# A token tower on one core: maxima rows by column transfers, k and q in one part, six of sixteen score slots written ahead by ScalarE, normalisation on VectorE in two pieces

## The chip, the core and the metric

The kernel runs on one core of a Trainium2 chip. Five engines work side by side: TensorE (PE, with its weight loads as PEld), VectorE (DVE), ScalarE (ACT), GpSimd (POOL) and SyncE (SP), which here only issues transfers. They share SBUF; TensorE writes to PSUM, which VectorE and ScalarE read. Each engine runs its own instructions in order and waits for the others by semaphores. The metric is the time of one execution in microseconds on the device, as the median of several.

## The reference

The input is 2 x 1024 token ids. What is computed, cut to what matters:

```
h = relu(conv(embedding(x)))                      # 2 x 1024 x 128
x = layernorm(h)
q, k, v = x Wq, x Wk, x Wv                        # 8 heads of 64
dots = q k^T * 64**-0.5
h = h + (softmax(dots) v) Wo + x
m = layernorm(h)
a = (layernorm(m) * g + b) Wa + ba + m
y = fc2_e(gelu(fc1_e(a)))                         # expert e by the token's place, 8 experts
h = h + gelu(y Wn + bn)
```

The softmax is the part around the change: each query's scores less their maximum over the keys go into the exponential.

## The kernel before

**Steps, parts, units.** A step s (0 to 7) is one pair of heads of one batch row. It has 16 units `(s, kc, half)`: key block kc (128 keys, 0 to 7) against query half (512 queries), both heads side by side, 128 x 1024 numbers in one PSUM slot. A step is worked in eight parts, two units in each; parts 0 to 3 take the query half 0, parts 4 to 7 the half 1 (`units_of`). In a part TensorE runs, in this order (`part_items`): a maximum item, two score items ("exp"), a second maximum item, what stands beside (`beside_values`), and then the values of the two units of the part before ("pv", line 524, into `acc_o`).

**Slots.** Three PSUM slots of two banks each go round all items that need one. Item n takes slot n % 3, and TensorE waits until the item three places earlier is released (line 572, `release`): an exp item by ScalarE's exponential (line 692), a maximum item by VectorE's reduction (line 847), a k or q item by VectorE's remainder (line 842).

**Scores** (`scores`, line 512) are four terms, each of two matmuls, one for each head: k_round x q_round, k_round x q_rest, k_rest x q_round and, as the fourth, a row of ones against `neg_rows`, which holds the negated maximum of each query. The sum is in PSUM when ScalarE takes the exponential.

**Maxima.** They are made a step ahead: "max" items multiply q_round with k_round (line 447), transposed, so that queries are partitions, and VectorE reduces along the keys (line 847). When four query blocks are done VectorE joins the two key halves into `maxes` (line 852, 128 x 8, both operands in SBUF). That happens in part 5 (for the next step, half 0) and in part 1 (for this step, half 1). A "rows" item, in parts 6 and 2, turns them: two transposes on TensorE (line 454), a negated copy by VectorE (`neg_max`, line 859), and two transfers on SP's queue (line 349) into the rows of `neg_rows`.

**k and q** of the next step are projected in part 0 (k) and part 1 (q): six matmuls each (line 440), rounded by ScalarE (line 697), remainder by VectorE (line 842).

**Denominators.** GpSimd adds up the exponentials (`add`, line 1026, 14 additions of 128 x 1024 a step). In part 3 TensorE sums step s - 1 over the partitions ("den", line 535), ScalarE copies (line 702), SP spreads the copy over 128 partitions (line 334), VectorE inverts (`invert`, line 880, last in its part 4), SP stores to DRAM (line 336) and loads it back, each row to 64 partitions (line 341, two transfers). GpSimd multiplies `attn_out` by it (`normalise`, line 1016) between its additions for kc 5 and 6 of half 1. Step 7's denominators come as "last den", one item for each half (lines 543, 871, 874).

**SP's queue** is one list, in order: the row transfers of half 1, the spread and its loads, the row transfers of the next step's half 0. In step 4 the first four experts' weights (line 355, 2 MB) stand between the first and the second of these; in step 6 the other four stand ahead of the last.

**Step 7** has, besides, the feed-forward layer's start: "wo" (line 462), the layer norm on VectorE (line 911), "nt" (line 469, which waits for it) and "xa". Behind it come the experts (lines 602, 613, 621).

The functions that the change touches, and what calls them:

Of the kernel before, what the change touches and what calls it, by code (L numbers as in the profile page):

```python
# [19 lines left out]
F32 = mybir.dt.float32  # L20
# [7 lines left out]
B, S = 2, 1024  # L28
# [23 lines left out]
AHEAD, ROWS_AT = 12, 9  # L52
# [7 lines left out]
PROLOGUE = ([("k", 0), ("q", 0)] + [("max", *m) for m in MAXES[:ROWS_AT]] + [("rows", 0, 0)]  # L60
            + [("max", *m) for m in MAXES[ROWS_AT:AHEAD]])
# [6 lines left out]
FFN_ITEMS = {(STEPS - 1, 0): [("wo",)], (STEPS - 1, 3): [("nt",)], (STEPS - 1, 5): [("xa",)], (STEPS - 1, 6): [("last den", 0)]}  # L68

# [18 lines left out]


def part_items(s, part):  # L90
# [3 lines left out]
    items += [("exp", *u) for u in units_of(s, part)] + maxes[1:] + beside_values(s, part)  # L94
# [19 lines left out]
NO_SLOT = ("pv", "o", "inv", "norms")  # L114
# [21 lines left out]
def unit(s, kc, half):  # L136

    return s * UNITS + half * KCH + kc

# [6 lines left out]
def build(nc, x, tables, w_in, wo_in, small_in, next_b, fc_in, out):  # L146
    VOCAB = VOCAB_ROWS
    with ExitStack() as ctx:
# [42 lines left out]
        with ExitStack() as att:  # L191
# [5 lines left out]
            def operands(p, scope):  # L197

                return [sb(f"{name}{p}", [128, S], F32R, scope) for name in ("q_round", "q_rest", "k_round", "k_rest", "neg_rows")]
# [3 lines left out]
            maxes = sb("maxes", [128, 2, KCH], F32, att)  # L203
            neg_max = sb("neg_max", [GROUP, 2, CHUNK], F32R, att)
            one_rows = sb("one_rows", [128, CHUNK], F32R, att)
            odd_operands = operands(1, att)

            with ExitStack() as early:
                xR = sb("xR", [C, B * S], F32R, early)
                xL = sb("xL", [C, B * S], F32R, early)  # L210
                q_round, q_rest, k_round, k_rest, neg_rows = zip(operands(0, early), odd_operands)
# [60 lines left out]
        rows_made = sem("rows_made")  # L272
        rows_loaded = sem("rows_loaded")
        summed = [[sem(f"summed_{p}_{half}") for half in ("low", "high")] for p in ("even", "odd")]
# [18 lines left out]
        def release(item):  # L293
# [8 lines left out]
            if kind == "rows":  # L302
                return rows_made, 2 * item[1] + item[2] + 1
# [12 lines left out]
        duo_slots, late_slot = (slots[FIRST_SLOT], slots[SUMS_SLOT]), slots[LATE_SLOT]  # L316
        inv_dram = nc.dram_tensor("inv_scratch", [128, 2 * S // 128], F32, kind="Internal").ap()
# [4 lines left out]
        def _(sp):  # L322
# [8 lines left out]
            def spread(s):  # L331
# [6 lines left out]
                if s > 0:  # L338
                    sp.wait_ge(normalised, s)
# [40 lines left out]
        def _(pe):  # L380
# [50 lines left out]
            def prep_item(item, slot):  # L431
# [10 lines left out]
                elif kind == "max":  # L442
# [7 lines left out]
                else:  # L450
                    half = item[2]
                    pe.wait_ge(max_joined, 2 * v + half + 1)
                    for h in range(2):
                        last = pe.transpose(slot[0:GROUP, h * BANK:h * BANK + CHUNK], maxes[:, h, half * GROUP:(half + 1) * GROUP],  # L454
                                            ident[:, :])
# [28 lines left out]
            def ffn_item(item, slot):  # L484

                kind = item[0]
                if kind == "wo":
                    pe.wait_ge(normalised, PAIRS)
# [11 lines left out]
            def scores(item, slot):  # L500
# [64 lines left out]
            for s in range(STEPS):  # L565
                for item, n in numbered(STEP_ITEMS[s], FIRST[s]):
# [5 lines left out]
                    pe.wait_ge(*release(ALL_ITEMS[n - SLOTS]))  # L572
# [55 lines left out]
            for half in range(2):  # L628
                pe.wait_ge(normalised, STEPS + half)
# [17 lines left out]
        def _(act):  # L647
# [85 lines left out]

            def o_copy(s, half):
# [18 lines left out]
            for s in range(STEPS):  # L753
                for item, n in numbered(STEP_ITEMS[s], FIRST[s]):
                    if item[0] == "o":
# [39 lines left out]
        def _(dve):  # L795
# [39 lines left out]
            def dve_item(item, n):  # L835
# [8 lines left out]
                elif kind == "max":  # L844
# [4 lines left out]
                    if qc % GROUP == GROUP - 1 and keys == 1:  # L849
                        own = slice(qc - GROUP + 1, qc + 1)  # L850
                        dve.wait_ge(maxed, MAXES.index(item[1:]) + 1)
                        dve.tensor_tensor(maxes[:, :, own], half_maxes[:, :, own, 0], half_maxes[:, :, own, 1],  # L852
                                          ALU.max).then_inc(max_joined, 1)
                elif kind == "rows":
                    _, v, half = item
                    dve.wait_ge(filled, n + 1)
                    if v + half > 0:
                        dve.wait_ge(rows_loaded, 32 * (2 * v + half))
                    dve.tensor_scalar(neg_max[:, :, :], slot[0:GROUP, :].rearrange("c (h n) -> c h n", h=2)[:, :, 0:CHUNK],
                                      -1.0, None, ALU.mult).then_inc(rows_made, 1)  # L860
# [4 lines left out]
                elif kind == "last den":  # L865
# [4 lines left out]
                    dve.wait_ge(normalised, STEPS - 1 + half)  # L870
# [42 lines left out]

            def dve_step(s):
                for item, n in numbered(STEP_ITEMS[s], FIRST[s]):
                    if item[0] == "inv":
                        invert(item[1])
# [172 lines left out]
```

## Time and profile before

| | us |
|---|---|
| median of 3 runs | 442.79 (442.66 to 442.96) |
| the profiled execution | 443.59 |
| its span, first to last instruction | 441.7 |

| engine | busy us | share of the span | instructions |
|---|---|---|---|
| PE | 417.8 | 95% | 2654 |
| PEld | 249.5 | 56% | 2654 |
| DVE | 252.7 | 57% | 327 |
| ACT | 204.5 | 46% | 285 |
| POOL | 300.8 | 68% | 148 |

The granted clock was 0.984 of full speed over the span. The time of matmuls overlaps: one pair begins before the last has ended, so neither the busy time nor the mean of one matmul is what a further one costs; the distance between starts is.

### The profile page before, as it was taken

Reading aid. Unit: us, or ns where it says so; the run is one execution under the profiler, and the core shown is the slowest. Engines: PE = TensorE matmul, PEld = TensorE weight load, DVE = VectorE, ACT = ScalarE, POOL = GpSimd, SP = SyncE. Lnnn points to the kernel's source line nnn. Section 1 sums busy time; section 2 is a strip of 40 time slices with the busy share of each in tenths; the row PEclk is TensorE's granted clock in tenths of the full one; section 3 lists DMA queues with packets and bytes.
Section 4 is the critical chain, followed back from the end, with each engine's and each line's share of the span. In section 5 each row is a group of like instructions: output and inputs, shape, how many; then the busy total and the mean of one; then the engine's idle time right before and its main releaser. Section 6 shows DMA issues by size and latency. Waiting matters only on the chain.

```text
span 441.7 us, 6550 instructions
## 1 busy us (share of the span) xinstructions
PE 417.8 (95%) x2654; PEld 249.5 (56%) x2654; DVE 252.7 (57%) x327; ACT 204.5 (46%) x285; POOL 300.8 (68%) x148
## 2 busy tenths in 40 slices
PE   7798899999999999999999999999999789697995
PEld 7675555555555455445544555454557335286994
DVE  1777675665658466755746575666654940356121
ACT  1455535354545445444544445454442634333663
POOL 3070278978898889879987988998794936900111
PEclk9989999999999999999999999999999979989999
DMA  6000000000100010020051000100330010000011
GB/s 228 1 1 1 0 2 1 2 0 3 49 2 0 3 48 1 2 49 2 1 193 48 2 0 3 48 2 0 100 142 0 2 48 4 0 1 1 19 30 49
DMA packets 7962, 12.03 MB, mean 27 GB/s; under 512 B 2684, under 2 KB 5244, under 8 KB 7932
## 3 DMA queue, kind: packets, MB, share of 16 engines
q1 hardware_dynamic: 7356, 10.63, 7.9%
q10 hardware_dynamic: 576, 0.98, 0.7%
q8 instruction: 21, 0.34, 0.3%
q14 instruction: 9, 0.07, 0.1%
HBM read 10.38 MB, written 1.11 MB: 26 GB/s over the span
## 4 chain that ended last, share of the span: by engine, by line
PE 85%; DVE 6%; POOL 2%; ACT 2%; issue 2%; DMA 1%; POOLq 0%; SPq 0%; ACTq 0%; DVEq 0%
PE acc_o L524 25%; PE slot L512 25%; PE slot L447 9%; PE slot L440 6%; PE slot L462 3%; PE slot L602 3%; PE acc_o L423 3%; PE acc_o L613 2%; DVE normed L911 2%; POOL sums L1026 2%; PE slot L535 2%; DMA residual<-in_x 1%; PE slot L454 1%; PE slot L478 1%; PE slot L399 1%
## 5 line engine op out<-in xcount | busy, mean ns | idle before, releaser
L1026 POOL TENSOR_TENSOR sums<-sums,probs 128x1024 f32<-128x1024 f32 x96 | 228.9, 2384 | 38.3 <-ACT probs L692 28.1
L847 DVE TENSOR_REDUCE half_maxes<-slot 128x2 f32<-128x1024 f32 x128 | 156.5, 1225 | 96.5 <-PE slot L447 96.1
L692 ACT ACTIVATE probs<-slot 128x1024 f32<-128x1024 f32 x128 | 124.9, 1025 | 131.4 <-PE slot L512 131.4
L524 PE MATMUL acc_o<-probs,v_all 128*64 128x512 f32 x512 | 124.1, 606 | 0.0
L524 PEld LDWEIGHTS acc_o<-probs,v_all 128*64 128x64 f32 x512 | 31.3, 136 | 60.4 <-issue 45.1
L1026 POOL TENSOR_TENSOR sums<-probs 128x1024 f32<-128x1024 f32 x16 | 38.2, 2389 | 32.3 <-ACT probs L692 32.3
L447 PE MATMUL slot<-k_round,q_round 64*128 64x512 f32 x256 | 57.7, 449 | 0.7 <-DVE half_maxes L847 0.7
L447 PEld LDWEIGHTS slot<-k_round,q_round 64*128 64x128 f32 x256 | 23.8, 183 | 53.2 <-issue 46.9
L512 PE MATMUL slot<-q_round,k_round 64*128 64x512 f32 x256 | 51.4, 397 | 1.2 <-DVE k_rest L842 1.0
L512 PE MATMUL slot<-q_round,k_rest 64*128 64x512 f32 x256 | 50.5, 390 | 0.0
L512 PE MATMUL slot<-q_rest,k_round 64*128 64x512 f32 x256 | 50.5, 390 | 0.0
L512 PE MATMUL slot<-neg_rows,one_rows 64*128 64x512 f32 x256 | 50.4, 388 | 0.0
L1042 POOL TENSOR_TENSOR probs<-probs,residual 128x256 f32<-128x256 f32 x8 | 5.8, 725 | 46.8 <-ACT probs L778 46.8
L512 PEld LDWEIGHTS slot<-q_round,k_round 64*128 64x128 f32 x256 | 24.1, 185 | 10.0 <-issue 4.9
L512 PEld LDWEIGHTS slot<-neg_rows,one_rows 64*128 64x128 f32 x256 | 24.1, 184 | 5.5
L512 PEld LDWEIGHTS slot<-q_round,k_rest 64*128 64x128 f32 x256 | 24.1, 184 | 5.5
L512 PEld LDWEIGHTS slot<-q_rest,k_round 64*128 64x128 f32 x256 | 24.1, 184 | 5.1
L771 ACT ACTIVATE probs<-slot,small 128x128 f32<-128x128 f32 x64 | 17.4, 383 | 18.1 <-PE slot L602 18.1
L871 DVE RECIPROCAL inv_sb<-slot 128x512 f32<-128x512 f32 x2 | 6.7, 3358 | 25.2 <-POOL attn_out L1016 22.5
L740 ACT COPY attn_out<-acc_o 128x512 f32<-128x512 f32 x14 | 8.2, 588 | 21.2 <-PE acc_o L524 21.2
L852 DVE TENSOR_TENSOR maxes<-half_maxes 128x8 f32<-128x8 f32 x16 | 17.6, 1103 | 0.6
L1016 POOL TENSOR_TENSOR attn_out<-attn_out,inv_sb 128x1024 f32<-128x1024 f32 x7 | 16.6, 2377 | 0.0
(114 smaller groups left out, 412.6 us busy)
## 6 DMA issues: line engine op xcount, KB each, us to landing
inv_sb<-inv_scratch SPq DMA_DIRECT2D x14, 256.0 KB, 3.9
v_all<-in_fc SPq DMA_DIRECT2D x4, 512.0 KB, 4.9
fc_late<-in_fc SPq DMA_DIRECT2D x4, 512.0 KB, 6.3
residual<-in_x SPq DMA_DIRECT2D x2, 512.0 KB, 5.9
out_h<-probs SPq DMA_DIRECT2D x8, 128.0 KB, 1.8
v_all<-in_w ACTq DMA_DIRECT2D x3, 256.0 KB, 7.4
neg_rows<-neg_max SPq DMA_DIRECT2D x32, 2.0 KB
woT<-in_wo SPq DMA_DIRECT2D x1, 256.0 KB, 7.7
```

The lines of the kernel that those rows point to most:

```text
L423: last = pe.matmul(bank(6 + t % 2), xs[:, rows], ws[:, :], start=(i == 0), stop=(i == 2))
L440: last = pe.matmul(slot[:, half * BANK:(half + 1) * BANK], ws[:, w, v % PAIRS, :], xs[:, cols], start=(i == 0), stop=(i == 2))
L447: last = pe.matmul(slot[:, h * BANK:(h + 1) * BANK], q_round[p][head_rows(h), qc * CHUNK:(qc + 1) * CHUNK], k_round[p][head_rows(h), half ...
L462: last = pe.matmul(slot[:, j * C:(j + 1) * C], attn_out[:, b * PAIRS + r, j * CHUNK:(j + 1) * CHUNK], woT[:, r, :], start=(r == 0), stop=( ...
L512: last = pe.matmul(slot[:, h * BANK:(h + 1) * BANK], stationary, qs[head_rows(h), cols], start=(i == 0), stop=(i == 3))
L524: last = pe.matmul(acc_o[head_rows(h), cols], v_all[:, s, kc, head_rows(h)], probs[unit(s, kc, half) % TILES][:, h, :], start=(kc == 0), s ...
L692: act.activation(probs[u % TILES][:, :, :].rearrange("p h n -> p (h n)"), slot[:, :], ACT.Exp, scale=SCALE).then_inc(exped, 1)
L771: act.activation(hidT[d % 2][:, i, r, :], slot[:, i, r], ACT.Gelu, bias=fc1_b_col[:, e * HC + r:e * HC + r + 1]).then_inc(hid_made, 1)
L847: dve.reduce_max(half_maxes[:, :, qc, keys], slot[:, :].rearrange("p (h n) -> p h n", h=2), AX.X).then_inc(maxed, 1)
L852: dve.tensor_tensor(maxes[:, :, own], half_maxes[:, :, own, 0], half_maxes[:, :, own, 1], ALU.max).then_inc(max_joined, 1)
L1016: pool.tensor_tensor(attn_out[:, s, :], attn_out[:, s, :], inv_sb[:, :], ALU.mult).then_inc(normalised, 1)
L1026: pool.tensor_tensor(sums[s % 2][half][:, :, :], before[:, :, :], probs[kc][:, :, :], ALU.add).then_inc(summed[s % 2][half], 1)
```

## The change

- **Rows by columns.** The "rows" items go, with their transposes, the copy by VectorE and `neg_max`. SP waits for the join and sends each column of `maxes` (128 numbers, one a partition) to its stretch of a row: eight transfers for each half instead of two. The row holds the maxima themselves, and the constant row is -1 instead of 1.
- **A plane.** When the eight have landed, SP stores the half's two rows to DRAM, waits, and loads them to all 128 partitions: `max_planes`, 128 x 1024. Both stand on SP's queue behind the columns, each behind a wait for the one before it.
- **Six of sixteen slots ahead.** For kc 2, 4, 6 of each half ScalarE writes minus the plane into the unit's slot ("fill"), at the end of the part before and behind that part's two exponentials. TensorE waits for it instead of for the slot's release, and runs three terms that add to it. It holds where the item three places earlier is an exp, max, k or q item: 47 units (six a step, five in step 7, in which (7, 2, half 1) keeps four terms).
- **k and q in one part.** Both stand in part 0.
- **Normalisation on VectorE.** GpSimd's 128 x 1024 multiplication is now two of 128 x 512 on VectorE, behind the second maximum of parts 5 and 7, and in step 7 both in part 6.

The diff, cut to its core:

```diff
-PROLOGUE = ([("k", 0), ("q", 0)] + [("max", *m) for m in MAXES[:ROWS_AT]] + [("rows", 0, 0)]
-            + [("max", *m) for m in MAXES[ROWS_AT:AHEAD]])
+PROLOGUE = [("k", 0), ("q", 0)] + [("max", *m) for m in MAXES[:AHEAD]]
...
+PREFILLED = (2, 4, 6)
...
-    if part < 2 and s + 1 < STEPS:
-        items.append(("kq"[part], s + 1))
-    if part == 2:
-        items.append(("rows", s, 1))
+    if part == 0 and s + 1 < STEPS:
+        items += [("k", s + 1), ("q", s + 1)]
     if part == 3 and s > 0:
         items.append(("den", s - 1))
-    if part == 6 and s + 1 < STEPS:
-        items.append(("rows", s + 1, 0))
...
-    items += [("exp", *u) for u in units_of(s, part)] + maxes[1:] + beside_values(s, part)
+    items += [("exp", *u) for u in units_of(s, part)] + maxes[1:]
+    beside = beside_values(s, part)
+    if s > 0:
+        items += [("norm", s - 1, i) for i, p in enumerate((5, 7) if s + 1 < STEPS else (6, 6)) if p == part]
+    items += beside
+    if part % 4 < 3:
+        items.append(("fill", *units_of(s, part + 1)[0]))
...
+WHOLE_SLOT = ("exp", "max", "k", "q")
+FILLED = [item[1:] for n, item in enumerate(ALL_ITEMS)
+          if item[0] == "exp" and item[2] in PREFILLED and ALL_ITEMS[n - SLOTS][0] in WHOLE_SLOT]
...
-                sp.wait_ge(rows_made, 2 * v + half + 1)
+                i = 2 * v + half
+                sp.wait_ge(max_joined, i + 1)
+                if i > 0:
+                    sp.wait_ge(rows_loaded, ROW_COUNT * i)
                 for h in range(2):
-                    sp.dma_start(neg_rows[v % 2][h * D:h * D + 1, half * BANK:(half + 1) * BANK].bitcast(F32)
-                                 .rearrange("a (c n) -> a c n", c=GROUP), neg_max[:, h, :].bitcast(F32)).then_inc(rows_loaded, 16)
+                    for c in range(GROUP):
+                        qc = half * GROUP + c
+                        sp.dma_start(max_rows_of[v % 2][h * D:h * D + 1, qc * CHUNK:(qc + 1) * CHUNK].bitcast(F32),
+                                     maxes[:, h, qc:qc + 1].bitcast(F32)).then_inc(rows_loaded, 16)
+                sp.wait_ge(rows_loaded, ROW_COUNT * (i + 1))
+                if i > 1:
+                    sp.wait_ge(plane_loaded, 16 * (i - 1))
+                sp.dma_start(rows_dram[half], max_rows_of[v % 2][0:128:D, half * BANK:(half + 1) * BANK].bitcast(F32)).then_inc(rows_stored, 16)
+                sp.wait_ge(rows_stored, 16 * i + 16)
+                if i > 1:
+                    sp.wait_ge(filled_in, filled_up_to(i - 2))
+                sp.dma_start(max_planes[half][:, :], rows_dram[half:half + 1].rearrange("a h n -> a (h n)").partition_broadcast(128)
+                             .rearrange("p a n -> p (a n)")).then_inc(plane_loaded, 16)
...
-                terms = ((k_round[p], q_round[p]), (k_round[p], q_rest[p]), (k_rest[p], q_round[p]), (one_rows, neg_rows[p]))
+                terms = [(k_round[p], q_round[p]), (k_round[p], q_rest[p]), (k_rest[p], q_round[p])]
+                ahead = item[1:] in FILLED
+                if not ahead:
+                    terms.append((minus_rows, max_rows_of[p]))
                 for i, (ks, qs) in enumerate(terms):
                     if i == 3 and kc == 0:
-                        pe.wait_ge(rows_loaded, 32 * (2 * s + half + 1))
+                        pe.wait_ge(rows_loaded, ROW_COUNT * (2 * s + half + 1))
                     for h in range(2):
                         stationary = ks[head_rows(h), :] if i == 3 else ks[head_rows(h), keys]
                         last = pe.matmul(slot[:, h * BANK:(h + 1) * BANK], stationary, qs[head_rows(h), cols],
-                                         start=(i == 0), stop=(i == 3))
+                                         start=(i == 0 and not ahead), stop=(i == len(terms) - 1), skip_group_check=ahead)
...
+                    if item[0] == "exp" and item[1:] in FILLED:
+                        pe.wait_ge(filled_in, FILLED.index(item[1:]) + 1)
+                    else:
+                        pe.wait_ge(*release(ALL_ITEMS[n - SLOTS]))
...
+            def fill(unit_item):
+
+                _, s, kc, half = unit_item
+                n = ALL_ITEMS.index(("exp", s, kc, half))
+                act.wait_ge(*release(ALL_ITEMS[n - SLOTS]))
+                act.wait_ge(plane_loaded, 16 * (2 * s + half) + 16)
+                act.activation(slots[n % SLOTS][:, :], max_planes[half][:, :], ACT.Copy, scale=-1.0).then_inc(filled_in, 1)
...
+                        turn = 2 * v + qc // GROUP
                         dve.wait_ge(maxed, MAXES.index(item[1:]) + 1)
+                        if turn > 1:
+                            dve.wait_ge(rows_loaded, ROW_COUNT * (turn - 1))
...
-                elif kind == "rows":
-                    _, v, half = item
-                    dve.wait_ge(filled, n + 1)
-                    if v + half > 0:
-                        dve.wait_ge(rows_loaded, 32 * (2 * v + half))
-                    dve.tensor_scalar(neg_max[:, :, :], slot[0:GROUP, :].rearrange("c (h n) -> c h n", h=2)[:, :, 0:CHUNK],
-                                      -1.0, None, ALU.mult).then_inc(rows_made, 1)
...
+            def normalise(s, half):
+
+                cols = slice(half * BANK, (half + 1) * BANK)
+                dve.wait_ge(inv_loaded, s * 32 + 32)
+                dve.tensor_tensor(attn_out[:, s, cols], attn_out[:, s, cols], inv_sb[:, cols], ALU.mult).then_inc(normalised, 1)
...
-            def normalise(s):
-
-                pool.wait_ge(inv_loaded, s * 32 + 32)
-                pool.tensor_tensor(attn_out[:, s, :], attn_out[:, s, :], inv_sb[:, :], ALU.mult).then_inc(normalised, 1)
...
-                        if half == 1 and kc == 5 and s > 0:
-                            normalise(s - 1)
...
```

## Rows read from the trace of the kernel before

**Rows 1.** The page, part 1 of PE and part 4 by engine

```profile
PE 417.8 (95%) x2654; PEld 249.5 (56%) x2654; DVE 252.7 (57%) x327; ACT 204.5 (46%) x285; POOL 300.8 (68%) x148
PE 85%; DVE 6%; POOL 2%; ACT 2%; issue 2%; DMA 1%; POOLq 0%; SPq 0%; ACTq 0%; DVEq 0%
```

**Rows 2.** Timeline, PE, step 3, part 4: start us, duration us, engine, line

```profile
189.43 0.50 PE L447 MATMUL slot<-k_round,q_round 64*128 64x512 f32 x2
189.76 0.39 PE L512 MATMUL slot<-q_round,k_round 64*128 64x512 f32 x2
190.68 0.40 PE L512 MATMUL slot<-q_round,k_round 64*128 64x512 f32 x2
191.91 1.94 PE L524 MATMUL acc_o<-probs,v_all 128*64 128x512 f32 x8
193.78 0.50 PE L447 MATMUL slot<-k_round,q_round 64*128 64x512 f32 x2
```

**Rows 3.** Timeline, PE: first maxima of parts 6, 7 and then 0, 1

```profile
198.14 0.50 PE L447 MATMUL slot<-k_round,q_round 64*128 64x512 f32 x2
202.88 0.50 PE L447 MATMUL slot<-k_round,q_round 64*128 64x512 f32 x2
207.27 0.51 PE L447 MATMUL slot<-k_round,q_round 64*128 64x512 f32 x2
213.25 0.50 PE L447 MATMUL slot<-k_round,q_round 64*128 64x512 f32 x2
```

**Rows 4.** Timeline, ACT in part 4 of step 3

```profile
190.90 1.94 ACT L692 ACTIVATE probs<-slot 128x1024 f32<-128x1024 f32 x2 [2.61 <-PE slot L512]
```

**Rows 5.** Timeline, DVE in parts 4 and 5 of step 3

```profile
193.17 0.24 DVE L880 RECIPROCAL inv_flat<-den_flat 128x16 f32<-128x16 f32 x1
...
196.38 1.23 DVE L847 TENSOR_REDUCE half_maxes<-slot 128x2 f32<-128x1024 f32 x1 [0.83 <-PE slot L447]
197.65 1.10 DVE L852 TENSOR_TENSOR maxes<-half_maxes 128x8 f32<-128x8 f32 x1
```

**Rows 6.** Timeline, POOL in parts 4 to 6 of step 3

```profile
192.91 2.39 POOL L1026 TENSOR_TENSOR sums<-probs 128x1024 f32<-128x1024 f32 x1 [1.07 <-ACT probs L692]
196.35 9.96 POOL L1026 TENSOR_TENSOR sums<-sums,probs 128x1024 f32<-128x1024 f32 x4 [1.05 <-ACT probs L692]
```

**Rows 7.** Timeline, SP's queue in parts 4 and 5 of step 3

```profile
188.31 0.57 SPq L334 DMA_DIRECT2D den_flat<-den_sb  x1
193.44 0.32 SPq L336 DMA_DIRECT2D inv_scratch<-inv_flat  x1
194.85 1.14 SPq L341 DMA_DIRECT2D inv_sb<-inv_scratch  x2
```

**Rows 8.** Issue to landing: page, part 6; tile v_all, SP's loads

```profile
inv_sb<-inv_scratch SPq DMA_DIRECT2D x14, 256.0 KB, 3.9
DMA to landing us min/median/max: 3.6/4.9/6.3
```

**Rows 9.** Line 852, DVE's join: duration ns min/median/max

```profile
L852 DVE TENSOR_TENSOR maxes<-half_maxes x16: 168/1102/2154, 42.0 to 343.9; 128x8 f32<-128x8 f32 x16
```

**Rows 10.** Timeline, SP's queue in step 4

```profile
224.72 1.86 SPq L355 DMA_DIRECT2D v_all<-in_fc  x4
```

**Rows 11.** Timeline, DVE and PE at the start of step 0

```profile
42.00 0.17 DVE L852 TENSOR_TENSOR maxes<-half_maxes 128x8 f32<-128x8 f32 x1
48.87 0.41 PE L512 MATMUL slot<-neg_rows,one_rows 64*128 64x512 f32 x2
```

**Rows 12.** Timeline, step 7 and its end

```profile
354.92 1.94 PE L535 MATMUL slot<-sums,ones 128*32 128x512 f32 x8 [4.22 <-DVE neg_max L859]
379.63 2.37 POOL L1016 TENSOR_TENSOR attn_out<-attn_out,inv_sb 128x1024 f32<-128x1024 f32 x1
382.10 3.36 DVE L871 RECIPROCAL inv_sb<-slot 128x512 f32<-128x512 f32 x1 [22.45 <-POOL attn_out L1016]
386.93 1.97 PE L543 MATMUL slot<-sums,ones 128*64 128x512 f32 x4 [4.05 <-POOL sums L1026]
```

More of the change, by code:

```diff
@@ L51 @@
 MAXES = [(v, qc, keys) for v in range(STEPS) for qc in range(KCH) for keys in range(2)]
-AHEAD, ROWS_AT = 12, 9
+AHEAD = 12
+ROW_COUNT = 16 * 2 * GROUP
 WARM_START, WARM_SPLIT = 24, 10
@@ L111, in step_items @@
     return items
-NO_SLOT = ("pv", "o", "inv", "norms")
+NO_SLOT = ("pv", "o", "inv", "norms", "norm", "fill")
 def numbered(items, first):
@@ L138, in unit, with filled_up_to @@
     return s * UNITS + half * KCH + kc
+WHOLE_SLOT = ("exp", "max", "k", "q")
+FILLED = [item[1:] for n, item in enumerate(ALL_ITEMS)
+          if item[0] == "exp" and item[2] in PREFILLED and ALL_ITEMS[n - SLOTS][0] in WHOLE_SLOT]
+def filled_up_to(turn):
+    return len([u for u in FILLED if 2 * u[0] + u[2] <= turn])
 def adds_done(s, kc):
@@ L197, in operands @@
             def operands(p, scope):
-                return [sb(f"{name}{p}", [128, S], F32R, scope) for name in ("q_round", "q_rest", "k_round", "k_rest", "neg_rows")]
+                return [sb(f"{name}{p}", [128, S], F32R, scope) for name in ("q_round", "q_rest", "k_round", "k_rest", "max_rows_of")]
             probs = [sb(f"probs{i}", [128, 2, BANK], F32, att) for i in range(TILES)]
             half_maxes = sb("half_maxes", [128, 2, KCH, 2], F32, att)
-            maxes = sb("maxes", [128, 2, KCH], F32, att)
-            neg_max = sb("neg_max", [GROUP, 2, CHUNK], F32R, att)
-            one_rows = sb("one_rows", [128, CHUNK], F32R, att)
+            maxes = sb("maxes", [128, 2, KCH], F32R, att)
+            max_planes = [sb(f"max_plane{i}", [128, 2 * BANK], F32, att) for i in range(2)]
+            minus_rows = sb("minus_rows", [128, CHUNK], F32R, att)
             odd_operands = operands(1, att)
@@ L210, in build @@
                 xL = sb("xL", [C, B * S], F32R, early)
-                q_round, q_rest, k_round, k_rest, neg_rows = zip(operands(0, early), odd_operands)
+                q_round, q_rest, k_round, k_rest, max_rows_of = zip(operands(0, early), odd_operands)
                 wR = sb("wR", [C, 2, PAIRS, 2 * D], F32R, early)
@@ L301, in release @@
                 return maxed, MAXES.index(item[1:]) + 1
-            if kind == "rows":
-                return rows_made, 2 * item[1] + item[2] + 1
             if kind == "wo":
@@ L338, in spread @@
                 if s > 0:
-                    sp.wait_ge(normalised, s)
+                    sp.wait_ge(normalised, 2 * s)
                 for h in range(2):
@@ L449, in prep_item @@
                                          k_round[p][head_rows(h), half * BANK:(half + 1) * BANK], start=True, stop=True)
[L450 to L455, printed above, removed]
                 last.then_inc(filled, 1)
@@ L628, in _ @@
             for half in range(2):
-                pe.wait_ge(normalised, STEPS + half)
+                pe.wait_ge(normalised, 2 * STEPS - 1 + half)
                 wo_half(1, half, late_slot).then_inc(wo_filled, 1)
@@ L754, in _ @@
                 for item, n in numbered(STEP_ITEMS[s], FIRST[s]):
-                    if item[0] == "o":
+                    if item[0] == "fill" and item[1:] in FILLED:
+                        fill(item)
+                    elif item[0] == "o":
                         o_copy(item[1], item[2])
@@ L869, in dve_item @@
                     dve.wait_ge(filled, n + 1)
-                    dve.wait_ge(normalised, STEPS - 1 + half)
+                    dve.wait_ge(normalised, 2 * (STEPS - 1) + half)
                     dve.reciprocal(inv_sb[:, cols], slot[:, 0:BANK]).then_inc(inverted, 1)
@@ L917, in dve_step @@
                         invert(item[1])
+                    elif item[0] == "norm":
+                        normalise(item[1], item[2])
                     elif item[0] == "norms":
```

14 lines of the change are left out of this document (7 added, 7 removed).

## The prediction

> **What bounds the kernel now.** I read the page's parts 1 and 4 first: TensorE is busy 95% of the span and is 85% of the chain that ended last [rows 1]. So a gain must come out of TensorE's list, and a loss comes from whatever makes it wait. What a matmul costs there I take from the timeline, since matmuls overlap. In part 4 of step 3 one score item follows the other after 190.68 - 189.76 = 0.92 us, for four terms [rows 2]: a term costs 0.23 us, though one of its matmuls lasts 0.39. The part lasts 193.78 - 189.43 = 4.35 us. Parts with more in them [rows 3]: part 6, which has a rows item, 4.74 us, so the item costs 0.39; part 0, which has k, 5.98 us. Then the timelines of the other engines in the same stretch [rows 4 to 7], to see how much room each has before TensorE needs it. I count in times from the start of the part: ScalarE's two exponentials run from 1.47 to 3.41 [rows 2, 4]; VectorE inverts the denominators at 3.74 [rows 2, 5].
>
> **What TensorE saves.** In each of steps 1 to 6: six fourth terms, 6 x 0.23 = 1.4 us, and two rows items, 0.8 us. That is 2.1 us of 40 (part 5 of one step to part 5 of the next). k and q side by side cost what they cost apart.
>
> **Does the fill come in time?** One row of an ordinary part answers. With three terms in its first score item the exponentials end at about 3.2 (the second waits for its own scores), and a copy of 128 x 1024 costs ScalarE about what an exponential does, 0.97 us [rows 4]: ready at 4.2. TensorE wants the slot 0.33 us [rows 2] into the next part, which begins at 4.12, so at 4.45. It is hidden, with 0.2 us to spare; if the copy cost 1.3 us it would cost 0.1 us, 47 times, 5 us. In part 0 the fill stands behind q's rounding; by the same counting it is 0.1 us late. VectorE has both remainders there too; with that I put down 0.2 us a step.
>
> **The plane.** Half 1's maxima are joined in part 1, some 12.4 us into the step. The issue of a row transfer takes SP about 0.57 us (the spread's [rows 7] is the nearest, 128 pieces too), so eight take 4.6; the store of the inverse took from its issue to the next issue 194.85 - 193.44 = 1.4 us [rows 7]; 512 KB landed 3.6 to 6.3 us after issue, where four such loads stood together [rows 8], the first soonest. So the rows are there at 12.4 + 4.6 + 1.4 = 18.4, the plane at 18.4 + 1.4 + 3.6 = 23.4. The first use of the row is at 22.1, that of the plane (end of part 4's exponentials) at 24.5. Both fit; the plane has 1 us. SP comes to the spread at 20.4 instead of 19.9, and the spread lands behind the plane, at 23.5 to 24; VectorE wants it at 24.8. If columns cost more, this is where it shows. Taken: nothing in steps 1 to 6. For half 0 there is 5 us more.
>
> **The normalisation, where the gain goes.** In the kernel before, GpSimd did it late in the half, and nobody waited. Now VectorE does, in its own list, behind the join of part 5, and ahead of part 6's first maximum. Behind the waiting instruction stands that maximum, and for its slot TensorE waits with part 6's second maximum item. Counted from the start of part 5 (193.78):
> - The inverse is asked for at 194.85 and 195.42 and lands 3.9 us later [rows 7, 8]: at 5.5. These steps hang on the inversion, which VectorE does at the same place as before, so this does not move.
> - GpSimd: the addition of kc 2 starts 2.57 into the part, behind the exponential [rows 6]; with three terms 2.3. One lasts 2.4, four in a row 9.96 [rows 6], so 2.49 apart: they end at 4.7 and 7.2.
> - VectorE's join starts at 3.87 and lasts 1.10, until 4.97, just when GpSimd's addition ends (196.35 + 2.39 = 198.74, and 197.65 + 1.10 = 198.75) [rows 5, 6]. The shortest join lasts 0.17 us, the longest 2.15, for the same eight numbers [rows 9]. I read this as a wait for GpSimd's running addition, which an operation with two operands in SBUF has to make. The normalisation is such an operation.
> - So it misses the gap at 4.7, starts at 7.2, takes between 0.5 and 0.7 (a 128 x 512 operation; half of the 1.23 of 128 x 1024 [rows 5]), and the maximum behind it ends at 7.2 + 0.6 + 1.23 = 9.0. TensorE wants the slot 6.05 into the part (4.12 + 0.33 + 1.6). It waits **3.0 us**.
>
> The second piece, in part 7, has its inverse but can meet an addition as well; I count 0.3 us at part 0's second maximum. Bounds of both together: 0.5 us, if the inverse lands before 4.7, to 5.4, if each meets a whole addition.
>
> The Trainium skill says the same of the lock ("SBUF — State Buffer", section "Who interferes with whom"): a `tensor_tensor` with both inputs in SBUF contends with GpSimd's reads, and the later one fully blocks. It speaks against this change. By that rule the stall is the 3.0 us above and the sum that of the forecast; without it the time is that of the second rival. The trace agrees, by the joins of 0.17 to 2.15 us.
>
> **Steps 1 to 6:** -2.1 + 3.0 + 0.3 + 0.2 = +1.4 us each, six times +8.4.
>
> **Step 4** more: the 2 MB of experts stood before the spread already, issued from 224.72 [rows 10]. They now stand behind the plane, 3 us later in the step, and land, with up to 6.3 us for one [rows 8], about 28.3 into it; the spread lands behind them, while VectorE waits at the inversion from 24.8. It holds part 5's maxima, and TensorE waits 2.5 us (0 to 3.5).
>
> **Step 0.** The first join ends at 42.17, the fourth term of the first unit ran at 48.87 [rows 11], and would run 0.3 earlier. Columns: 42.2 + 4.8 + 1.4 = 48.4, just in time. The first plane lands at 53.4, before ScalarE can use it; half 1's plane comes about 1 us late. Of 2.3 us of savings 1.0 us is left.
>
> **Step 7 and the end.** TensorE waited 4.22 us for the negated copy, which stood behind the second layer norm on VectorE, and then ran the denominators for 1.94 us [rows 12] and "nt", which needs that norm. Without the copy the denominators run inside the wait, and "nt" begins about 2.2 us sooner. At the end the chain goes through GpSimd's last additions, in which its normalisation of 2.37 us stood [rows 12], between two of them; TensorE's last sum at 386.93 waited for the additions. It is gone: 2.4 us. With one term, 0.2: -4.8 us. The 22.45 us for which VectorE waited there [rows 12] are no gain beyond this, since the next on the chain is the last sum.
>
> **Sum:** -1.0 + 8.4 + 2.5 - 4.8 = +5.1. The profiled execution has a span of 441.7 and took 443.59; the median of the runs is 442.79, 0.8 below. From the median: **447.9 us**.
>
> **Rivals.**
> 1. *The inverse is in time.* If it lands before the addition of kc 2 ends, join and normalisation share a gap: 0.5 us instead of 3.0, and with the phase so shifted the piece in part 7 is free. Then -1.4 a step, -8.4: in all -11.7, **431 us**. For it: 5.5 against 4.7 is close. Against: even with the second load landing 3.5 us after its issue it is 5.1. Chance 0.17.
> 2. *No lock for this operation.* VectorE waits for the inverse only: 5.5 + 0.7 + 1.23 = 7.5, stall 1.4; -0.5 a step: **437 us**. For it: the join is tiny, and could wait for its own operands instead. Against: its end falls on the addition's end. Chance 0.08.
> 3. *TensorE saves it all*, because the landing is earlier than I read or the wait has more room: about -18, **425 us**. Chance 0.09.
> 4. *The columns are slow* (slower still). They are pieces of 4 bytes, where the spread's have 64. It decides from 1 us more for the chain of eight on: at 2 us more TensorE waits 0.7 us a step at the first filled unit of half 1, +5, **453 us**; at 4 us more 2.7 a step, 467. Nothing in the trace shows such pieces. Chance 0.16.
> 5. *It does nothing*: gains and waits cancel within 0.2%, which is about what a measurement of this kernel can tell. The forecast's sum is 5 us of terms that are 8 and 5 large. Chance 0.05.
>
> The forecast keeps 0.45. Range: 430 to 457 leaves out most of 3 (0.09) and the far part of 4 (0.07) and a few hundredths on the near side, under 0.2. Its own range for the forecast is 443.5 to 452. Faster 0.17 + 0.08 + 0.09 + 0.01 = 0.35, same 0.05, slower 0.6.
>
> **What would show it.** The distance of two "den" items (L535) in the timeline, 40.0 now: 41.4 by the forecast, 38.6 by the first rival, 37.9 by the third. Who waited for whom: TensorE on the reductions of line 847, six times about 3 us, at part 6's second maximum. VectorE's normalisation: a mean well above 0.7 us, with its end on the end of an addition. Behind the loads of the planes, VectorE's inversion without a wait save in step 4. On ScalarE a fill of about 1.0 us. If TensorE waits for fills instead, the columns or the copy were mis-sized; if it waits for nothing and the step is 38 us, the wait for the inverse was.

## The result and the profile after

| | before | after |
|---|---|---|
| median, us | 442.79 (442.54 to 442.96, 5 runs) | 449.04 (447.11 to 449.66, 5 runs) |
| ratio | | 1.0129, 95% interval 1.0115 to 1.0144 |
| the profiled execution, us | 443.59 | 447.11 |
| its span, us | 441.7 | 445.3 |

Slower by 1.3%, with less work on TensorE: busy 405.0 us instead of 417.8 [rows 1]. The profiled execution is the fastest of the five, 1.9 us below the median. The page of the changed kernel, parts 1, 4, 5 and 6 (line, engine, operation, output and input, count; busy us, mean ns of one; idle us before it and what ended that; at the end the transfers' KB and us to landing):

```profile
PE 405.0 (91%) x2528; PEld 241.3 (54%) x2528; DVE 266.3 (60%) x325; ACT 251.0 (56%) x332; POOL 287.8 (65%) x141
PE 66%; DVE 12%; DMA 11%; SPq 3%; ACT 3%; POOL 2%; issue 2%; POOLq 0%; ACTq 0%
...
L476 PE MATMUL slot<-k_round,q_round 64*128 64x512 f32 x256 | 59.8, 466 | 19.7 <-DVE half_maxes L886 19.5
L769 ACT ACTIVATE slot<-max_plane 128x1024 f32<-128x1024 f32 x47 | 48.3, 1028 | 3.4 <-DMA max_plane<-rows_scratch 1.7
L953 DVE TENSOR_TENSOR attn_out<-attn_out,inv_sb 128x512 f32<-128x512 f32 x14 | 22.9, 1642 | 16.3 <-DMA inv_sb<-inv_scratch 16.3
...
max_plane<-rows_scratch SPq DMA_DIRECT2D x16, 512.0 KB, 3.5
inv_sb<-inv_scratch SPq DMA_DIRECT2D x14, 256.0 KB, 3.9
max_rows_of<-maxes SPq DMA_DIRECT2D x128, 0.5 KB, 2.0
```

The chain has moved: TensorE had 85% of it [rows 1], now 66; VectorE has 12% and transfers 11%, the loads of the inverse foremost. TensorE waits for VectorE's maxima (L886), 19.5 us in all. The piece of the normalisation (L953) lasts 1.64 us in the mean, and for the same 128 x 512 0.69 where nothing is in its way (below).

The place itself, in step 3, parts 5 and 6, from the timelines of TensorE, VectorE, GpSimd and SP's queue:

```profile
192.81 0.50 PE L476 MATMUL slot<-k_round,q_round 64*128 64x512 f32 x2
...
196.97 0.50 PE L476 MATMUL slot<-k_round,q_round 64*128 64x512 f32 x2
...
201.81 0.51 PE L476 MATMUL slot<-k_round,q_round 64*128 64x512 f32 x2 [2.73 <-DVE half_maxes L886]
```

```profile
196.48 1.10 DVE L894 TENSOR_TENSOR maxes<-half_maxes 128x8 fp32r<-128x8 f32 x1
198.47 2.15 DVE L953 TENSOR_TENSOR attn_out<-attn_out,inv_sb 128x512 f32<-128x512 f32 x1 [0.90 <-DMA inv_sb<-inv_scratch]
200.55 1.21 DVE L886 TENSOR_REDUCE half_maxes<-slot 128x2 f32<-128x1024 f32 x1
...
195.17 10.18 POOL L1064 TENSOR_TENSOR sums<-sums,probs 128x1024 f32<-128x1024 f32 x4 [0.51 <-ACT probs L721]
...
193.91 1.15 SPq L355 DMA_DIRECT2D inv_sb<-inv_scratch  x2
```

Part 5 starts at 192.81. GpSimd's additions start at 195.17 and stand some 2.5 apart, so there are gaps at about 197.6 and 200.1. The join ends at 197.58, in the first. The inverse lands at 198.47, 5.66 into the part, too late for that gap; the piece ends at 200.6, in the next. Then comes part 6's first maximum, until 201.76, and TensorE, which wanted its slot 2.73 us before, goes on at 201.81. The same wait, 2.70 to 2.73 us, stands in steps 1, 2, 3, 5 and 6. It is the gap that sets it, and not how late the inverse is: in step 2 the inverse landed 1.2 us later (6.9 into the part), just ahead of the same gap. The piece then took only 0.89 us and TensorE waited as long (VectorE and TensorE, step 2):

```profile
158.84 0.89 DVE L953 TENSOR_TENSOR attn_out<-attn_out,inv_sb 128x512 f32<-128x512 f32 x1 [2.15 <-DMA inv_sb<-inv_scratch]
160.92 0.49 PE L476 MATMUL slot<-k_round,q_round 64*128 64x512 f32 x2 [2.71 <-DVE half_maxes L886]
```

From den item to den item (TensorE's timeline; 40.0 us from each to the next up to step 6 before):

| stretch | before | after | difference | forecast |
|---|---|---|---|---|
| start to step 1's | 106.6 | 102.4 | -4.2 | -1.9 |
| 1 to 2 | 40.0 | 42.3 | +2.3 | +1.4 |
| 2 to 3, 3 to 4 | 80.0 | 81.8 | +1.8 | +2.8 |
| 4 to 5 | 40.0 | 46.3 | +6.3 | +3.9 |
| 5 to 6 | 40.0 | 42.5 | +2.5 | +1.4 |
| 6 to the end | 135.1 | 130.1 | -5.1 | -2.5 |
| sum | 441.7 | 445.3 | +3.6 | +5.1 |

The sum is that of the two profiled executions. The medians are 6.2 us apart, and no trace shows the other 2.6.

### The profile page after: what moved, and what is told of

The parts are those of the page before. It is cut to its first block, busy times and chain, and to the rows that moved or that the text cites. A ratio compares the mean times of both kernels' runs of the same rounds, so it can differ in the third digit from the quotient of the medians.

```text
span 445.3 us, 6537 instructions
## 1 busy us (share of the span) xinstructions
PE 405.0 (91%) x2528; PEld 241.3 (54%) x2528; DVE 266.3 (60%) x325; ACT 251.0 (56%) x332; POOL 287.8 (65%) x141
## 4 chain that ended last, share of the span: by engine, by line
PE 66%; DVE 12%; DMA 11%; SPq 3%; ACT 3%; POOL 2%; issue 2%; POOLq 0%; ACTq 0%
PE acc_o L550 18%; PE slot L538 17%; PE slot L476 8%; DMA inv_sb<-inv_scratch 6%; PE slot L468 5%; DVE half_maxes L886 4%; PE slot L485 3%; PE slot L631 3%; PE acc_o L642 2%; DVE attn_out L953 2%; POOL sums L1064 2%; DVE normed L946 2%; SPq L368 2%; DMA inv_scratch<-inv_flat 2%; PE acc_o L412 2%
## 5 line engine op out<-in xcount | busy, mean ns | idle before, releaser
L1064 POOL TENSOR_TENSOR sums<-sums,probs 128x1024 f32<-128x1024 f32 x96 | 232.0, 2417 | 68.1 <-ACT probs L721 57.5
L886 DVE TENSOR_REDUCE half_maxes<-slot 128x2 f32<-128x1024 f32 x128 | 156.3, 1224 | 81.8 <-PE slot L476 81.5
L721 ACT ACTIVATE probs<-slot 128x1024 f32<-128x1024 f32 x128 | 124.5, 1024 | 110.4 <-PE slot L538 110.4
L550 PE MATMUL acc_o<-probs,v_all 128*64 128x512 f32 x512 | 127.3, 620 | 0.0
L476 PE MATMUL slot<-k_round,q_round 64*128 64x512 f32 x256 | 59.8, 466 | 19.7 <-DVE half_maxes L886 19.5
L1064 POOL TENSOR_TENSOR sums<-probs 128x1024 f32<-128x1024 f32 x16 | 38.2, 2390 | 19.0 <-ACT probs L721 18.3
L769 ACT ACTIVATE slot<-max_plane 128x1024 f32<-128x1024 f32 x47 | 48.3, 1028 | 3.4 <-DMA max_plane<-rows_scratch 1.7
L953 DVE TENSOR_TENSOR attn_out<-attn_out,inv_sb 128x512 f32<-128x512 f32 x14 | 22.9, 1642 | 16.3 <-DMA inv_sb<-inv_scratch 16.3
L538 PE MATMUL slot<-max_rows_of,minus_rows 64*128 64x512 f32 x162 | 32.1, 390 | 0.3 <-DMA max_rows_of<-maxes 0.3
L538 PEld LDWEIGHTS slot<-max_rows_of,minus_rows 64*128 64x128 f32 x162 | 15.3, 184 | 4.0 <-DMA max_rows_of<-maxes 0.8
L881 DVE TENSOR_TENSOR k_rest<-slot,k_round 128x1024 fp32r<-128x1024 f32 x8 | 9.8, 1225 | 10.0 <-ACT k_round L726 9.9
L894 DVE TENSOR_TENSOR maxes<-half_maxes 128x8 fp32r<-128x8 f32 x16 | 15.1, 945 | 0.6
```

What stands on the lines that cost most here:

```text
L476: last = pe.matmul(slot[:, h * BANK:(h + 1) * BANK], q_round[p][head_rows(h), qc * CHUNK:(qc + 1) * CHUNK], k_round[p][head_rows(h), half ...
L550: last = pe.matmul(acc_o[head_rows(h), cols], v_all[:, s, kc, head_rows(h)], probs[unit(s, kc, half) % TILES][:, h, :], start=(kc == 0), s ...
L721: act.activation(probs[u % TILES][:, :, :].rearrange("p h n -> p (h n)"), slot[:, :], ACT.Exp, scale=SCALE).then_inc(exped, 1)
L769: act.activation(slots[n % SLOTS][:, :], max_planes[half][:, :], ACT.Copy, scale=-1.0).then_inc(filled_in, 1)
L886: dve.reduce_max(half_maxes[:, :, qc, keys], slot[:, :].rearrange("p (h n) -> p h n", h=2), AX.X).then_inc(maxed, 1)
L953: dve.tensor_tensor(attn_out[:, s, cols], attn_out[:, s, cols], inv_sb[:, cols], ALU.mult).then_inc(normalised, 1)
```

## The experiments

The theory: VectorE's piece in part 5 costs the time, by the late inverse and GpSimd's running addition together. The rivals: one of these two alone; the columns, planes and fills; for step 4 the transfers' traffic. The kernel before, run beside them, took 442.7 to 442.8 us; the ratios are against it.

**Normalisation back on GpSimd.**

```diff
-                        normalise(item[1], item[2])
+                        pass
...
+            def normalise(s):
+                pool.wait_ge(inv_loaded, s * 32 + 32)
+                pool.tensor_tensor(attn_out[:, s, :], attn_out[:, s, :], inv_sb[:, :], ALU.mult).then_inc(normalised, 2)
...
+                        if half == 1 and kc == 5 and s > 0:
+                            normalise(s - 1)
```

(VectorE passes over its two pieces, GpSimd has the multiplication back.)

> The changed kernel with the normalisation back on GpSimd as one 128 x 1024 multiplication behind kc 5 of half 1; columns, planes, filled slots and k with q stay. Theory (VectorE's piece in part 5, late inverse and GpSimd's addition, holds part 6's first maximum and with it TensorE): the waits of 2.7 us at part 6 are gone in steps 1 to 3 and 5 and 6, and in step 4 its second one of 2.0; the distance of two den items falls from 40.9 to 38.0; step 4's first wait (experts ahead of the spread) stays; GpSimd's 2.4 us come back at the end. 449.0 - 13.6 - 2.0 - 4.5 (slow clock behind the waits) + 2.4 = about 431 us. Rival (columns, planes and fills cost what the change loses): the steps stay at 40 to 41, 440 us or more.

Measured: 431.8 us, ratio 0.972 (0.966 to 0.978). The den distance is 37.7 us in four of five steps (44.3 in step 4), 38.0 was expected, 37.9 by the prediction's third rival; no wait at part 6 is left. TensorE's wait in part 5 of step 4 stays (2.97 us), and behind it the granted clock was 0.50 over 4 us. So the rest of the change works as computed, and 17 us lie in the place of the normalisation.

**The lock alone, taken away.**

```diff
-                dve.tensor_tensor(attn_out[:, s, cols], attn_out[:, s, cols], inv_sb[:, cols], ALU.mult).then_inc(normalised, 1)
+                dve.reduce_max(norm_dummy[:, ...], inv_sb[:, cols]..., AX.X).then_inc(normalised, 1)
```

> The multiplication is left out: in its place, at the same place and behind the same wait for the inverse, stands a reduction of 128 x 512 from SBUF, with one operand; attention is not normalised, except in step 7. Theory (an operation with two operands in SBUF waits for GpSimd's running addition): the piece lasts about 0.6 us instead of 2, TensorE's wait at part 6 falls from 2.7 to 1.3 us, part 7's piece costs nothing; five steps x 1.4, fewer stretches at the slow clock: 439 to 442 us. Rival (only the late inverse matters): the piece still ends with GpSimd's addition or costs as much, 449 us as before.

Measured: 436.8 us, ratio 0.985 (0.980 to 0.990). VectorE's and TensorE's timelines in step 3:

```profile
194.91 0.69 DVE L954 TENSOR_REDUCE norm_dummy<-inv_sb 128x2 f32<-128x512 f32 x1 [0.91 <-DMA inv_sb<-inv_scratch]
...
196.78 0.50 PE L477 MATMUL slot<-k_round,q_round 64*128 64x512 f32 x2 [1.26 <-DVE half_maxes L887]
```

With one operand in SBUF the piece lasts 0.69 us behind the same wait for the inverse, and TensorE's wait is 1.26 to 1.93 us. The rival "only the late inverse" falls: the second operand, of both pieces together, is worth 12 us.

**The inverse alone, taken away.**

```diff
-                    sp.wait_ge(normalised, 2 * s)
+                    sp.wait_ge(inv_loaded, 32 * s)
...
-                dve.wait_ge(inv_loaded, s * 32 + 32)
-                dve.tensor_tensor(..., attn_out[:, s, cols], inv_sb[:, cols], ALU.mult)
+                if s == STEPS - 2:
+                    dve.wait_ge(inv_loaded, s * 32 + 32)
+                dve.tensor_tensor(..., attn_out[:, s, cols], fixed[:, cols], ALU.mult)
```

> The pieces multiply by a fixed tile instead of the inverse and wait for no transfer (step 6's wait alone stays, since inv_sb is written behind it); attention is not normalised, except in step 7. Theory: the piece goes in the same gap between two additions as the join, part 6's wait falls from 2.7 to about 0.4 us, also in step 4, where only part 5's wait of 3 us stays: 449.0 - 5 x 2.3 - 2.0 - 4.3 = about 431 us. Rival (the lock alone makes the wait, whatever the inverse does): the piece waits for a whole addition still, 449 us. Rival (columns or fills): 440 us or more.

Measured: 430.4 us, ratio 0.972 (0.967 to 0.977). VectorE's timeline in step 3:

```profile
191.26 0.68 DVE L955 TENSOR_TENSOR attn_out<-attn_out,fixed 128x512 f32<-128x512 f32 x1
```

Both operands are in SBUF, GpSimd adds on, and the piece lasts 0.68 us: it follows the join in the same gap. Of the wait at part 6 0.28 us is left (den distance 38.2). The rival "the lock makes the wait, whatever the inverse does" falls too. It needs both.

**The real inverse, sooner.** VectorE inverts behind the first maximum of part 4 and no longer behind the second.

```diff
-    items = maxes[:1]
+    items = maxes[:1] + [("inv", s - 1)] * (part == 4 and s > 0)
```

(and "inv" no longer at the end of part 4)

> VectorE inverts behind the first maximum of part 4 instead of behind the second, 2.0 us sooner; nothing else. Theory: the inverse lands 3.6 us into part 5, ahead of the gap at 4.7, so join and piece share it; part 6's wait falls from 2.7 to about 0.4 us, the den distance from 40.9 to 38.6. In step 4 the inversion waits for the experts' transfers and now holds part 4's second maximum, 2 us more than before. About 434 us. Rival (the wait is GpSimd's addition whatever the inverse does, or columns and fills): 445 us or more.

Measured: 439.2 us, ratio 0.991 (0.988 to 0.995); 434 was expected, a miss by 5. The profiled execution took 443.8 us and holds both cases. VectorE and TensorE in step 2, and then in step 5:

```profile
157.65 1.07 DVE L894 TENSOR_TENSOR maxes<-half_maxes 128x8 fp32r<-128x8 f32 x1
158.79 0.69 DVE L953 TENSOR_TENSOR attn_out<-attn_out,inv_sb 128x512 f32<-128x512 f32 x1
...
160.68 0.51 PE L476 MATMUL slot<-k_round,q_round 64*128 64x512 f32 x2 [0.42 <-DVE half_maxes L886]
...
275.03 0.25 DVE L915 RECIPROCAL inv_flat<-den_flat 128x16 f32<-128x16 f32 x1 [0.83 <-DMA den_flat<-den_sb]
280.43 1.09 DVE L894 TENSOR_TENSOR maxes<-half_maxes 128x8 fp32r<-128x8 f32 x1
281.70 2.88 DVE L953 TENSOR_TENSOR attn_out<-attn_out,inv_sb 128x512 f32<-128x512 f32 x1 [0.17 <-DMA inv_sb<-inv_scratch]
...
285.76 0.80 PE L476 MATMUL slot<-k_round,q_round 64*128 64x512 f32 x2 [2.73 <-DVE half_maxes L886]
```

Where the inverse was there when the join ended, the piece took 0.69 us and TensorE waited 0.42; where it came 0.17 us late, the piece took 2.88 and TensorE waited 2.73. That happened in steps 1, 5 and 6 (late by 0.66, 0.17 and 0.34 us). The price of being late is a wait until the next gap, however small the lateness. My expectation had the landing at 3.6 into part 5 and the gap at 4.7. In those three steps it landed at 4.9 to 5.4. What failed is the 2 us: the denominators' spread had not landed where VectorE now wanted it, so the inversion waited 0.7 to 1.1 us in steps 1, 2, 3, 5 and 6, and came only 0.9 to 1.3 us sooner. That left next to nothing of the margin, and the scatter of the landing decided. In step 4 the inversion waited 7.68 us, and TensorE 3.96 instead of the changed kernel's 3.06. How many steps are late in an execution of 439 us no trace shows.

**The first piece one part later.**

```diff
-        items += [... enumerate((5, 7) if s + 1 < STEPS else (6, 6)) if p == part]
+        items += [... enumerate((6, 7) if s + 1 < STEPS else (6, 6)) if p == part]
```

> The changed kernel with the first piece of the normalisation one part later, behind part 6's second maximum, when the inverse has landed long since. Theory (late inverse and GpSimd's addition both count): no wait for the inverse, but the piece meets a running addition, ends with it and holds part 7's first maximum: TensorE waits some 1.2 us at part 7's second maximum instead of 2.7 at part 6's. 449.0 - 5 x 1.5 - 2.0 (step 4) - 4.3 (slow clock) = about 435 us. Rival (only the inverse is late): no wait, 429 us. Rival (columns, planes, fills): 445 us or more.

Measured: 438.9 us, ratio 0.990 (0.988 to 0.993). The timeline in step 3:

```profile
198.17 2.65 DVE L953 TENSOR_TENSOR attn_out<-attn_out,inv_sb 128x512 f32<-128x512 f32 x1
...
202.01 0.50 PE L476 MATMUL slot<-k_round,q_round 64*128 64x512 f32 x2 [1.10 <-DVE half_maxes L886]
```

Without any wait for the inverse the piece lasts 2.65 us, and TensorE waits 1.10 us, as expected; I had not counted that the second piece then lasts 2.40 and costs 0.6 more in each step (den distance 39.9).

**This one part of the change on the kernel before.** The edit is that of the change's own diff for the two pieces and what waits for them, and nothing else of it.

> The kernel before with this one part of the change alone: GpSimd's normalisation becomes VectorE's two pieces in parts 5 and 7 (in step 7 both in part 6). Theory: the same wait appears, 2.6 to 3 us at part 6 of each of six steps, den distance 42.6 or more instead of 40.0; 2.4 us gained at the end: 442.8 + 6 x 2.8 - 2.4 + up to 4 for the slow clock behind the waits = 457 to 461 us. Rival (the pieces only hurt together with filled slots and planes): 443 us or less.

Measured: 465.8 us, ratio 1.052 (1.049 to 1.055), slower than the whole change. Step 3:

```profile
208.37 2.18 DVE L921 TENSOR_TENSOR attn_out<-attn_out,inv_sb 128x512 f32<-128x512 f32 x1 [0.88 <-DMA inv_sb<-inv_scratch]
...
211.75 0.50 PE L450 MATMUL slot<-k_round,q_round 64*128 64x512 f32 x2 [2.49 <-DVE half_maxes L850]
```

457 to 461 was expected. The wait is 2.5 us in each of six steps, a little less than expected, but the den distance is 44.5: behind each of the six waits TensorE ran at the lower clock for a while (granted clock 0.57 to 0.61 over 4 us; some 1.7 us of TensorE's time each, 10 in all, where I had up to 4). The rival, that pieces only hurt beside fills and planes, falls.

**The experts' loads behind the spread.**

```diff
-                if s == PAIRS:
-                    sp.wait_ge(pv_done, unit(PAIRS, 0, 0))
-                    load_experts(EARLY_EXPERTS, fc_loaded[0])
                 if s > 0:
                     spread(s - 1)
+                if s == PAIRS:
+                    sp.wait_ge(pv_done, unit(PAIRS, 0, 0))
+                    load_experts(EARLY_EXPERTS, fc_loaded[0])
```

> The changed kernel with the first four experts' loads behind the spread of the denominators in step 4 instead of ahead of it. Theory: VectorE's wait of 5.5 us at the inversion goes, with it TensorE's of 3.1 us in part 5 and that of 0.9 for the fill; step 4 takes 40.9 instead of 46.3 us: about 444 us. Rival (step 4's loss is something else, such as the transfers' traffic): step 4 stays at 46 us.

Measured: 445.0 us (441.1 to 447.3), ratio 1.0045 (1.001 to 1.008), 4.0 below the changed kernel's 449.0 (447.1 to 449.7). What goes is this (changed kernel, step 4: SP's queue, VectorE, TensorE):

```profile
229.82 2.05 SPq L383 DMA_DIRECT2D v_all<-in_fc  x4
231.91 0.63 SPq L348 DMA_DIRECT2D den_flat<-den_sb  x1
...
238.70 0.25 DVE L915 RECIPROCAL inv_flat<-den_flat 128x16 f32<-128x16 f32 x1 [5.52 <-DMA den_flat<-den_sb]
...
240.09 0.51 PE L476 MATMUL slot<-k_round,q_round 64*128 64x512 f32 x2 [3.06 <-DVE half_maxes L886]
```

Neither the wait of 5.52 us nor that of 3.06 stands in the new trace; part 6's does, 2.73 us until 243.56. Step 4 still takes 43.8 us in its profiled execution, 3.0 over the 40.8 from step 2 to 3 and from 3 to 4. It is the lower clock, which lasted twice as long as behind the other waits (7 us of this run; the number before the last two is the granted clock, 0.52):

```profile
243.00:250.00 7.00, 6.44 (x22) 2.74 (x24) 2.95 (x3) 0.05 (x1) 3.92 (x2) 0.52 0.40 101
```

At half speed from 243.6 to 249.6 TensorE did 3 us of work less.

**Both together.** The normalisation on GpSimd and the experts' loads behind the spread.

> Both mends: normalisation on GpSimd and the experts' loads behind the spread; columns, planes, filled slots and k with q stay. Theory: every step 37.7 us, step 4 too; 431.8 less 5 to 6.6 is about 426 us, the best so far. Rival (waits only move): 431 us.

Measured: **425.2 us**, ratio 0.961 (0.959 to 0.964): every step 37.7 us (step 4: 38.3). It beats both kernels.

**What a fill buys**, on that version (`PREFILLED = ()`):

> The version with both mends (normalisation on GpSimd, experts behind the spread), but no slot is filled ahead: all units run four terms, no copies on ScalarE; the planes are still loaded. Theory (a term costs the 0.23 us between starts, not the 0.39 that one matmul lasts): 47 x 0.23 = 10.8 us more, den distance 39.1 instead of 37.7, 436 us; a fill costs TensorE nothing. Rival (a term costs what a matmul lasts): 47 x 0.39 = 18 us more, 443 us. Rival (fills cost as much as they save): 425 us.

Measured: 435.0 us, ratio 0.983 (0.981 to 0.986); den distance 39.1, 1.4 us more for six terms, 0.23 each. 47 fills are worth 9.8 us. In steps 1 to 6 of the version with fills they cost TensorE nothing; at its two ends TensorE does wait for them, 1.61 and 0.37 us in step 0, 1.05 and 0.41 in step 7.

**What k with q buys**, on the same version:

```diff
-    if part == 0 and s + 1 < STEPS:
-        items += [("k", s + 1), ("q", s + 1)]
+    if part < 2 and s + 1 < STEPS:
+        items.append(("kq"[part], s + 1))
```

> The version with both mends, with q's projection back in part 1; 47 slots are filled as before. Theory (k and q side by side cost what they cost apart): den distance 37.7 us as before, 425 us within 1. Rival (the pair delays VectorE's remainders or the fill): up to 0.3 us a step, 2 us less.

Measured: 433.7 us, ratio 0.981 (0.977 to 0.985), 8.5 us worse. 425 within 1 was expected: a plain miss. Step 3, VectorE and TensorE in part 1 and 2:

```profile
170.31 2.38 DVE L894 TENSOR_TENSOR maxes<-half_maxes 128x8 fp32r<-128x8 f32 x1
172.61 1.21 DVE L881 TENSOR_TENSOR q_rest<-slot,q_round 128x1024 fp32r<-128x1024 f32 x1
...
173.88 0.50 PE L538 MATMUL slot<-q_round,k_round 64*128 64x512 f32 x2 [0.23 <-DVE q_rest L881]
```

With q in part 1 its remainder stands behind the join, which waits a whole addition for eight numbers (2.38 us), and the slot behind the remainder. In part 0 there is no join. The den distance is 38.6 instead of 37.7, and in step 4 41.0, where column transfers issued behind the experts' loads also landed late. So k with q is worth 7 to 8.5 us on this version (6.8 between the two profiled executions, 8.5 between the medians), where I had put nothing.

## Why the prediction was right, point by point

- **TensorE's savings**: 2.1 us a step forecast (1.38 and 0.78, so 2.2), 40.0 - 37.7 = 2.3 measured without the pieces, and nothing of the 0.2 that I had put down for part 0. The price of a term, 0.23 and not 0.39, holds (no fills: 1.4 us for six). That of k with q was wrong as a statement: apart they cost 0.9 more in this kernel, whose slots are filled ahead.
- **The fill**: 1.028 us, hidden in steps 1, 2, 3, 5 and 6, as forecast. Elsewhere TensorE waited for fills: 1.61 us in part 0 of step 0, where the fill stands behind the rounding of k and q (0.1 forecast; the kernel before waited 0.99 there, for k's remainder), 0.94 in step 4, 1.04 and 0.41 in step 7, for which the forecast had nothing. **The columns**: 5.0 us for eight issues and 2.0 to landing, 1.0 more than the 6.0 that I took (4.6 and 1.4; the sum for step 0 has 4.8 for the same eight, a slip); the row's first use waited 0.3 us in step 0 and nowhere else. **The plane** landed 3.5 us after its issue (3.6 taken). The fourth rival, which was to decide from 1 us more on, is thereby out, and only just: in step 3 the plane had landed 0.6 us before ScalarE began the fill (187.75 + 3.5 against 191.88), and step 4's plane, beside the experts, did hold a fill for 1.32 us.
- **The wait at part 6**: 3.0 forecast, 2.73 measured, with each time of its working found: inverse at 5.66 (5.5), gap at 4.8 (4.7), next at about 7.3 (7.2). It is shown to need both causes, by two runs that each take one away. The second rival (no lock) falls by the reduction. The first (inverse in time) was 0.9 us away at its nearest, by the row of step 3; the earlier inversion shows that it would have held had the inverse come that much sooner.
- **The second piece**: it lasted 1.73 us, and costs at most the 0.5 us by which 40.9 exceeds 37.7 + 2.7. The forecast had 0.3 and 0.2.
- **Step 4**: mis-sized, +3.9 forecast and +6.3 measured. VectorE waited 5.52 us where I had 3.5, since the den copy left SP 2 us behind the experts and landed last. But of TensorE's waits little came of it: 0.94 for the fill, 3.06 in part 5 and 1.97 in part 6 are 6.0 us, and the forecast had 2.5 + 3.0 = 5.5. Most of what was missing is the lower clock behind the wait of 3.06 us (0.63 over 4 us, 1.7 us of TensorE's time).
- **Step 7 and the end**: GpSimd's multiplication of 2.4 us is gone, as forecast. The wait of 4.22 us [rows 12] is gone too, and with it what I had not seen in the row beside it: the denominators took 1.94 us there and take 1.06 now. That was the lower clock behind the wait; "nt" had it as well (1.97, now 1.06). It makes most of the 2.6 us by which this stretch beat the forecast. That was luck: the prediction's working has no clock in it.
- **What was missing from the sum**: the clock behind the new waits, some 1.4 to 1.7 us a time, in two of the five steps with equal waits and in step 4. That and the rest of step 4 are on one side, start (-2.3, of which 1.2 is a stretch of lower clock at 21 to 25 us that the profiled execution of before had and that of the changed kernel had not) and end on the other. So the total was nearer (447.9 against 449.0) than its terms, and that is luck; the direction and the place of the loss are not.

## What to carry to other kernels

An operation moved to an idle engine carries its waits into that engine's order: ask which instruction stands behind it, and which slot that holds. Here an operation with two SBUF operands on VectorE and GpSimd's additions took turns by whole instructions, so being 0.17 us late cost TensorE 2.3 us (a wait of 2.73 instead of 0.42); either share a gap, or keep the operation on the engine that already does the long ones. And test the parts of a change one by one: here all but the normalisation were worth 11.0 us (431.8 against 442.8), and 17.6 with a reordered load (425.2), and the normalisation alone cost 17.2 (449.0 against 431.8).

## What the runs showed of the hardware that was not expected

The clock behind a short wait. The changed kernel's granted clock (PEclk) in 4 us behind the waits of steps 1 and 2, and TensorE's timeline in step 1:

```profile
core 0: us, PE busy (x) PEld busy (x) DVE busy (x) ACT busy (x) POOL busy (x), PEclk, DMA share, GB/s
118.40:122.40 4.00, 3.84 (x12) 1.14 (x12) 1.33 (x2) 0.00 (x0) 3.54 (x2) 0.59 0.06 1
160.80:164.80 4.00, 3.88 (x24) 2.00 (x26) 2.34 (x3) 0.35 (x1) 3.52 (x2) 1.00 0.06 1
```

```profile
118.56 0.79 PE L476 MATMUL slot<-k_round,q_round 64*128 64x512 f32 x2 [2.70 <-DVE half_maxes L886]
119.29 3.10 PE L550 MATMUL acc_o<-probs,v_all 128*64 128x512 f32 x8
```

Behind two equal waits of 2.7 us the clock was 0.59 of full speed over 4 us once, which is the lower level of 1.2 GHz (0.50) for most of it, and 1.00 the other time. The eight matmuls took 3.10 us instead of 1.94. In this trace it followed two of five such waits, and that of 3.06 us in step 4; on the kernel before with the two pieces all six of 2.5 us. The length of the wait does not decide it. In the traces with the reduction and with the later piece the waits of 1.1 to 1.9 us never brought it, but in that of the earlier inversion one of 1.62 us in step 0 did (0.60 from 56 to 60 us), and a wait of 3.41 us in step 4 with the fixed tile did not (1.00 over 4 us). Why one wait brings it and another does not stayed open.

It is probably also part of why the changed kernel scatters (447.1 to 449.7) where the one before does not (442.5 to 443.0). Of the ten runs with the experts behind the spread the two at a mean granted clock of 0.989 took 441.1 and 441.9 us, the four at 0.977 446.0 to 447.3. In the five of the changed kernel (0.974 to 0.986) the order is not so clean: 448.3 us at 0.986, 447.1 at 0.982.

The Trainium skill ("SBUF — State Buffer", section "SBUF: two separate sides") calls the shared ports an exclusive lock, held for the whole instruction. The runs agree: 0.69 us for the piece in a gap, up to 2.88 beside an addition.
